# One core, cross attention and a binary-weight FFN in fp32: the FFN steps, the value products and the rotations in another order within a slot

## The reference

```python
q = (query @ Wq) ; k = (key @ Wk) ; v = (value @ Wv)      # query = layernorm(x), key = value = ctx
q = q * cos + _rotate_half(q) * sin                       # rotary, the same for k
attn = softmax(where(mask == 0, -1e9, q @ k.T / sqrt(128)))
x = x + (attn @ v) @ Wo
# FFN on y = layernorm(x)
routing = softmax(y @ gate_w.T)                           # 8 experts
in_scale, out_scale = routing @ in_channel_scale, routing @ out_channel_scale
x = x + (y * in_scale @ sign(weight).T * out_scale + bias)
```

## Time and profile before

| | us |
|---|---|
| median of 3 runs | 1142.5 |
| lowest, highest | 1142.41, 1143.6 |
| the profiled execution | 1143.86 |
| its span, first to last instruction | 1142.1 |
| PE busy in the span | 1131.5 |
| DVE, POOL, ACT busy | 814.2, 704.8, 537.4 |

### The profile page before, as it was taken

One profiled execution on the slowest core, in us unless ns is written; L12 is line 12 of the kernel. 1 busy time (PEld: TensorE's weight loads), 2 busy tenths in 40 slices (PEclk: granted clock), 3 DMA queues, 4 the chain that ended last, 5 costly groups with the idle time before them and its releaser, 6 DMA issues.

```text
span 1142.1 us, 22918 instructions
## 1 busy us (share of the span) xinstructions
PE 1131.5 (99%) x7927; PEld 954.3 (84%) x7927; DVE 814.2 (71%) x1366; ACT 537.4 (47%) x1736; POOL 704.8 (62%) x585
## 2 busy tenths in 40 slices
PE   8999999999999999999999999999999999999998
PEld 8788888888888888888888888888888888888877
DVE  5876877667677766877767776677766767776577
ACT  4554453544444354454554435544444544445533
POOL 5856676655667556675565676566674656755544
PEclk9999999999999999999999999999999999999999
DMA  8323342233323123332422323333232222322301
GB/s 250 113 80 98 106 133 84 83 102 89 97 69 113 61 92 94 105 116 88 115 86 69 99 81 87 91 106 107 84 93 74 75 85 73 89 77 74 93 20 38
DMA packets 134483, 105.29 MB, mean 92 GB/s; under 512 B 10680, under 2 KB 109256, under 8 KB 134400
## 3 DMA queue, kind: packets, MB, share of 16 engines
q1 hardware_dynamic: 128848, 93.72, 28.0%
q10 hardware_dynamic: 4784, 8.40, 2.2%
q0 software_dynamic: 768, 2.10, 0.6%
HBM read 100.00 MB, written 4.19 MB: 91 GB/s over the span
## 4 chain that ended last, share of the span: by engine, by line
PE 92%; DVE 3%; issue 2%; ACT 1%; POOL 1%; DMA 1%; ACTq 0%; DVEq 0%; POOLq 0%
PE chunk L1262 22%; PE chunk L1264 21%; PE chunk L1263 21%; PE duo_ps L1339 6%; PE o_ps L1362 3%; PE duo_ps L1251 2%; PE aux L1251 2%; PE duo_ps L1362 2%; DVE swp L945 1%; PE chunk L1315 1%; PE o_ps L1317 1%; PE o_ps L1316 1%; PE chunk L1317 1%; PE o_ps L1315 1%; PE chunk L1316 1%
## 5 line engine op out<-in xcount | busy, mean ns | idle before, releaser
L455 POOL TENSOR_TENSOR w_lo<-raw,w_hi 128x512 fp32r<-128x512 f32 x192 | 247.6, 1303 | 313.5 <-ACT w_hi L597 311.3
L945 DVE TENSOR_TENSOR swp<-chunk,sinT 64x512 f32<-64x512 f32 x320 | 220.2, 688 | 49.5 <-PE chunk L1264 29.9
L597 ACT ACTIVATE w_hi<-raw 128x512 fp32r<-128x512 f32 x192 | 116.6, 630 | 269.1 <-PE chunk L1264 202.4
L1262 PE MATMUL chunk<-xT_hi,w_hi 128*128 128x512 f32 x508 | 205.0, 404 | 0.6 <-POOL w_lo L455 0.6
L1264 PE MATMUL chunk<-xT_hi,w_lo 128*128 128x512 f32 x508 | 198.7, 391 | 0.0
L1263 PE MATMUL chunk<-xT_lo,w_hi 128*128 128x512 f32 x508 | 198.1, 390 | 0.0
L1262 PE MATMUL chunk<-wo_hi,oT_hi 128*128 128x512 f32 x492 | 195.1, 396 | 0.2 <-DVE oT_lo L879 0.2
L1264 PE MATMUL chunk<-wo_hi,oT_lo 128*128 128x512 f32 x492 | 191.9, 390 | 0.0
L1263 PE MATMUL chunk<-wo_lo,oT_hi 128*128 128x512 f32 x492 | 191.7, 390 | 0.0
L634 ACT ACTIVATE probs<-scores,neg_max 128x64 f32<-128x64 f32 x512 | 170.4, 337 | 42.5 <-DVE neg_max L901 42.5
L462 POOL TENSOR_TENSOR qT<-qT,swp 128x512 f32<-128x512 f32 x127 | 164.1, 1300 | 35.9 <-DVE qT L947 35.3
(11 more groups left out here) (305 smaller groups left out, 2045.8 us busy)
## 6 DMA issues: line engine op xcount, KB each, us to landing
raw<-in_L_xattn_Wq SPq DMA_DIRECT2D x128, 256.0 KB, 2.8
raw<-in_L_xattn_Wo SPq DMA_DIRECT2D x128, 256.0 KB, 2.7
raw<-in_L_xattn_Wk SPq DMA_DIRECT2D x32, 256.0 KB, 2.8
raw<-in_L_xattn_Wv SPq DMA_DIRECT2D x32, 256.0 KB, 3.0
acc<-in_x ACTq DMA_DIRECT2D x14, 256.0 KB, 2.7
x_tile<-in_x SPq DMA_DIRECT2D x12, 256.0 KB, 2.9
c_tile<-in_ctx SPq DMA_DIRECT2D x12, 256.0 KB, 3.2
result<-y ACTq DMA_DIRECT2D x12, 256.0 KB, 2.0
```

The costliest lines, as they stand in the source:

```text
L455: nc.gpsimd.tensor_tensor(lo, raw[:, r, :], hi.bitcast(F32), ALU.subtract).then_inc(wsplit_lo, 1)
L597: return nc.scalar.activation(dst, src, ACT.Copy)
L945: last = nc.vector.tensor_tensor(swp[to, k, :], bank[of, :], sinT[to, here], ALU.mult)
L1262: nc.tensor.matmul(bank, a_hi, b_hi, start=opens and i == 0, stop=False)
```

## The change

On PE, an even slot did projection 2, the values, the routing transpose, projection 3, the in-scales, projection 4, the out-scales, the value rows' first half, the sign product, the second half. It now does projections 2 and 3, the routing transpose, projection 4, the values, the in-scales, first half, out-scales, second half, sign product. In odd slots the out-scale product stands right behind the in-scales and goes to the bank `o_ps[1]`, which the attention values used, so it waits for `out_lo` of tile 1; ACT copies it from there. The second bank of the value rows is `chunk[1]` in place of `o_ps[0]`, and in odd slots `out_proj(s, 0)` follows the scores.

On DVE, `v_lo_split` moves from the odd slot's beginning to the even slot's end; the odd tile's `f_stats` and `f_norm` move into the even slot, around `rotate(s, 1)`; in even slots `out_lo` stands behind all rotations; in odd slots with an FFN tile `rotate(s, 1)` stands behind `scale_in`; in slot 31 `rotate(s, 0)` stands ahead of `pT_lo_split`. On POOL, in even slots rotation sums and splits alternate, and `xs_lo_split` stands behind `split_lo(s, 9)`. At the start four of six idle products go, three `split_lo` go from POOL to DVE, and one value weight is loaded by ACT's queue in place of SP's. In the last attention `out_proj(s, 3)` is cut after two heads instead of three.

```diff
-        V_BANK, FIRST_V_BANK = [chunk[1], o_ps[0]], [chunk[0], sc_ps]
+        V_BANK, FIRST_V_BANK = [chunk[0], chunk[1]], [chunk[0], sc_ps]
...
                     rope_sum(s, 0)
                     split_lo(s, 6 if s.odd else 5)
+                    if s.ffn and not s.odd:
+                        f_root(f[0] + 1, in_slot)
                     rope_sum(s, 1)
-                    if not s.odd:
-                        split_lo(s, 6)
+                if s.proj and s.odd:
                     split_lo(s, 7)
-                if s.ffn:
-                    xs_lo_split(f[0], in_slot)
-                if s.proj:
+                    if s.ffn:
+                        xs_lo_split(f[0], in_slot)
                     split_lo(s, 8)
                     rope_sum(s, 2)
...
                 if s.proj and not s.odd:
+                    split_lo(s, 6)
+                    rope_sum(s, 2)
+                    split_lo(s, 7)
+                    rope_sum(s, 3)
+                    split_lo(s, 8)
+                    rope_sum(s, 4)
                     split_lo(s, 9)
+                    if s.ffn:
+                        xs_lo_split(f[0], in_slot)
                     split_lo(s, 10)
-                    rope_sum(s, 3)
-                    rope_sum(s, 4)
...
                 if s.odd:
-                    rotate(s, 0)
+                    if s.number != SLOTS - 1:
+                        rotate(s, 0)
                     if s.ffn:
                         route_lo(f[0], in_slot)
                     if s.intake:
                         x_lo_split(*t)
-                    rotate(s, 1)
+                    if not s.ffn:
+                        rotate(s, 1)
                     out_lo(s, 0)
                     out_lo(s, 1)
                     if s.ffn:
                         scale_in(f[0], in_slot)
+                        rotate(s, 1)
                     rotate(s, 2)
...
+                    if s.ffn:
+                        f_stats(f[0] + 1, f[1] + 1, in_slot)
                     rotate(s, 1)
                     if s.ffn:
-                        route_lo(f[0], in_slot)
+                        f_norm(f[0] + 1, f[1] + 1, in_slot)
                     if s.intake:
                         x_lo_split(*t)
                     rotate(s, 2)
+                    rotate(s, 3)
+                    if s.ffn:
+                        route_lo(f[0], in_slot)
+                    rotate(s, 4)
+                    if s.ffn:
+                        scale_in(f[0], in_slot)
                     out_lo(s, 0)
-                    if s.ffn:
-                        scale_in(f[0], in_slot)
-                    rotate(s, 3)
                     out_lo(s, 1)
...
                 if not s.odd:
-                    rotate(s, 4)
+                    v_lo_split(s, 0)
+                    v_lo_split(s, 1)
...
+                for n in range(WRING):
+                    dve.wait_ge(wsplit_hi, n + 1)
+                    lo_of(flat(w_lo[:, n, :, :]), raw[:, n, :], flat(w_hi[:, n, :, :])).then_inc(wsplit_lo, 1)
...
+            def t_out_scales_apart(s, f, b, bank):
+
+                pe.wait_ge(o_lo, (s.U - 1) * PAIRS + 2)
+                nc.tensor.matmul(bank[:, :], b.routeT, out_sc[:, :], start=True, stop=True).then_inc(osc_done, 1)
...
                 if s.odd:
+                    project(s, 1)
+                    values(s, 0)
+                    values(s, 1)
+                    if s.ffn:
+                        t_route(f, in_slot)
+                    project(s, 2)
+                    if s.ffn:
+                        t_in_scales(f, in_slot)
+                        t_out_scales_apart(s, f, in_slot, o_ps[1])
+                    project(s, 3)
                     project(s, 4)
+                    if s.ffn:
+                        t_product(f, in_slot)
                 else:
+                    project(s, 2)
+                    project(s, 3)
+                    if s.ffn:
+                        t_route(f, in_slot)
+                    project(s, 4)
+                    values(s, 0)
+                    values(s, 1)
+                    if s.ffn:
+                        t_in_scales(f, in_slot)
                     v_rows(s, 0)
-                if s.ffn:
-                    t_product(f, in_slot)
-                if not s.odd:
+                    if s.ffn:
+                        t_out_scales(f, in_slot)
                     v_rows(s, 1)
+                    if s.ffn:
+                        t_product(f, in_slot)
...
-                idle_products(6)
+                idle_products(2)
```

More of the change, by code:

```diff
@@ L379, in load_weights @@
                         sp.wait_ge(wsplit_lo, split_count(s, n) - RING)
-                    if is_proj(c):
+                    if s.first_proj and c == V_OWN:
+                        pass
+                    elif is_proj(c):
                         src = (wk_c[:, :, bass.ts(grp, D)] if c == 0 else
@@ L1063, in slot @@
                     return scales_lo()
-                if s.odd:
-                    even = Slot(s.q, s.g - 1, False, False, odd=0)
-                    v_lo_split(even, 0)
-                    v_lo_split(even, 1)
                 if s.intake:
@@ L1083, in slot @@
                 if s.odd:
+                    add_out(s, 0)
+                    soft_b(s, 0)
                     add_out(s, 1)
-                soft_b(s, 0)
-                add_out(s, 2)
-                add_out(s, 3)
-                soft_b(s, 1)
-                if not s.odd:
+                    add_out(s, 2)
+                    soft_b(s, 1)
+                    add_out(s, 3)
+                    if s.number == SLOTS - 1:
+                        rotate(s, 0)
+                else:
+                    soft_b(s, 0)
+                    add_out(s, 2)
+                    add_out(s, 3)
+                    soft_b(s, 1)
                     rotate(s, 0)
@@ L1279, in out_proj @@
                     pe.wait_ge(added, (s.U - 3) * PAIRS + p + 1)
+                elif p < 2 and s.odd:
+                    pe.wait_ge(v_ok, s.U + p)
                 elif p == 0:
                     pe.wait_ge(cos_done, (s.U - 1) * KQ + 3)
-                elif p == 1 and s.odd:
-                    pe.wait_ge(v_ok, s.U)
                 elif p == 1:
@@ L1453, in attend_last @@
                 probs_T(s, 0)
-                out_proj(s, 3, range(HG - 1))
+                out_proj(s, 3, range(HG // 2))
                 values(s, 0)
-                out_proj(s, 3, range(HG - 1, HG))
+                out_proj(s, 3, range(HG // 2, HG))
                 probs_T(s, 1)
@@ L1490, in slot @@
                 t, f = (job and job[0] for job in jobs_of(s)[:2])
-                out_proj(s, 0)
                 if not s.odd:
+                    out_proj(s, 0)
                     out_proj(s, 1)
@@ L1500, in slot @@
                 if s.ffn:
-                    t_f(f, in_slot)
+                    t_f(f, in_slot, s.odd)
                 if s.odd:
+                    out_proj(s, 0)
                     out_proj(s, 1)
```

63 lines of the change are left out of this document (28 added, 35 removed).

## The result

| | before | after |
|---|---|---|
| median of 5 runs each on the same chip, us | 1142.5 | 1148.07 |
| lowest, highest | 1142.33, 1143.6 | 1147.17, 1149.13 |
| the profiled execution, its span | 1143.86, 1142.1 | 1149.13, 1147.3 |

The ratio is 1.0049, with a 95% interval of [1.0038, 1.0061]: the changed kernel is slower by 5.6 us, beyond the 0.2% of the prediction's text. The forecast was 1147.3, with a range of 1144.4 to 1149.8. The spans of the two profiles differ by 5.2 us.

A forecast was written before the change was run, and what follows sets the result against it. PE's stream was taken to bound the kernel, so only its waits count: +7.2 (odd slots) - 0.6 (even) - 0.6 (start) - 1.2 (end) = +4.8 us on 1142.5, giving 1147.3, range 1144.4 to 1149.8.

The forecast's parts named there:

- Odd slots, the largest term: Odd FFN slots: sign product waits for in-scales, scale_in, moved rotation and three POOL operations; 1.2 us each, +7.2 in six.
- makes projection 4 wait for the rotation of head 1, which is about nothing: Odd FFN slots: rotation ready at 390.93 against projection 4's start at 390.94, so taken as 0.
- Even slots with an FFN tile: Waits and returns saved (-0.22, -0.2) against new waits (+0.1, +0.2): -0.1 us a slot, -0.6 in six.
- Slots without an FFN tile: 0: Order changes, but no wait before and over 1 us of room in the same chains: 0.
- The return into the projections: Even FFN slots: in-scales right behind the values save one such return on PE, 0.2 us.
- The start: Program start: fewer idle products let first keys start sooner, partly at slow pace; -0.6 us, bounds 0 and 1.0 of gain.
- they stay covered: Start: DVE splits push x's statistics by about 2 us, hidden since PE transposes x only after 36 value matmuls.
- The end: Slot 31 and last attention: rotate(s, 0) in DVE's idle time gains 1.0, earlier out_proj cut 0.2; -1.2 us.
- lose the race to POOL: Even-slot rival: POOL's sum goes before f_norm, in-scales come 1.0 us later, six slots add 6.0; 1153.3 us, chance 0.15.
- The faster rival: Odd slots: the sign product does not wait, leaving -3.0; 1139.5 us, chance 0.10.
- The half wait: Odd slots: PE reaches the product later for other reasons, +3.6 instead of +7.2; 1143.7 us, chance 0.10.
- The start at the lower pace: Start rival: twelve key matmuls at the lower clock level, +1.1 instead of -0.6; 1149.0 us, chance 0.07.

The follow-up runs named there:

- experiment 1: Changed kernel with POOL doing split_lo 7 and xs_lo_split ahead of rope_sum 1 in odd slots with an FFN tile: 1141.03 us.
- experiment 2: Changed kernel with rotate(s, 1) of odd FFN slots back ahead of the two out_lo: 1146.48 us.
- experiment 3: Changed kernel with split_lo 8 also ahead of xs_lo_split on POOL in odd FFN slots: 1160.03 us.
- experiment 4: Kernel before with only the odd FFN slot's tail changed: rotate(s, 1) behind scale_in, out-scales behind in-scales in o_ps[1]'s bank: 1151.03 us.
- Experiment 10: Kernel of experiment 1 with the value weight's load on SP's queue and, in even FFN slots, xs_lo_split ahead of split_lo 9: 1139.23 us.
- experiment 8: Kernel of experiment 1 with the whole start of the kernel before (idle products, splits on POOL, load on SP's queue): 1141.38 us.
- experiment 9: Kernel of experiment 1 with the last slot's rotate(s, 0) back behind the routing: 1142.21 us.
- experiment 5: Kernel of experiment 1 with the first load of the own value weight back on SP's queue: 1140.33 us.
- experiment 12: Changed kernel with split_lo 8 and rope_sum 2 both ahead of xs_lo_split in odd FFN slots: 1170.97 us.
- experiment 6: Kernel of experiment 1 with the first three split_lo back on POOL instead of DVE: 1141.31 us.
- experiment 7: Kernel of experiment 1 with six idle products ahead of the first keys instead of two: 1141.2 us.

## Why the prediction was right, and where it was not

**Odd slots, the largest term: right in mechanism, 1 us too small.** Predicted 6 x 1.2 = +7.2, measured 6 x 1.37 = +8.2. The mis-sized term is the hand-overs from engine to engine: 0.25 in the sum, and 0.04, 0.03, 0.14 and 0.15 in the rows, 0.36 in all, the two at POOL the long ones. With it the chain from the in-scales to the product is 7.50 us, where the sum had 7.41 (387.48 to 394.89). Another 0.07 lies behind the product: its first step is 0.31 instead of 0.23. Beside this one step of the text failed without being paid for here: "makes projection 4 wait for the rotation of head 1, which is about nothing". Two times that agreed to 0.01 us were in truth a wait of 0.22: the matmul came 0.13 us behind the end of the rotation, and both the step to it and the one behind it were 0.1 too long. The chain covers this wait in the changed kernel; experiment 1 pays it, 6 x 0.24 = 1.4 us. Experiments 1 to 4 show the chain from each side.

**Even slots with an FFN tile: right**, -0.6 predicted and -0.7 measured. Experiment 10 shows that the wait for `xs_l` in it was real, at the 0.2 predicted.

**"Slots without an FFN tile: 0": wrong by a little.** The nine even ones behind the start are shorter by 0.05 to 0.09 us, 0.7 in all. The return into the projections that was counted in slots with an FFN tile is part of it: in slot 4 three projections in one piece take 8.38 us, where they took 8.52 in two pieces. The first keys of slot 2 and of the next slot start at 70.68 and 107.01 before, at 70.29 and 106.53 after: 36.33 and 36.24 apart.

**The start: its size is near, its reasoning failed.** Predicted -0.6; the two profiles reach the first keys of slot 2 (70.68 and 70.29) 0.39 apart, and by experiments 1 and 8 the start is worth 0.35. The step that failed is "they stay covered". It counted the splits on DVE, which push the statistics back, but not the DMA that the change puts ahead of x tiles 0 and 2 on ACT's queue. Nor was the profile of before a typical start: with the same code, experiment 4 gets out of it 1.5 us sooner (69.22). The gain was sooner keys and no wait for lo parts, the loss a pause at x of up to 1.1 us.

**The end: right**, -1.2 predicted and -1.1 measured (from the last projecting slot's keys to the end 67.45 before and 66.36 after, by spans of 1142.06 and 1147.32); experiment 9 gives the rotation's part, 0.86 in the pause.

Sum of the profiles: +8.2 - 0.7 - 0.7 - 0.4 - 1.1 = +5.3, against +4.8 predicted and 5.2 between the spans.

**The rivals.** `f_norm` did not lose the race to POOL in any even slot: it took 0.54 in all six. The faster rival, in which the product does not wait, did not come. Experiment 1 made it true and landed at 1141.0, where this rival had 1139.5: it took 0.1 off each odd slot, and projection 4's wait adds 0.24. The half wait did not come either. The start at the lower pace did not decide the profiled execution of the changed kernel, whose first four keys took 1.20 us; it exists in part in the profile of the kernel before (1.67), and in full in those of experiments 5 and 9 (2.08).

## What to carry to other kernels

When an operation is moved behind another on one engine, look at what the next engine's fixed order has queued behind its partner. Here POOL idled 3.17 us in front of a sum that nobody needed yet, with an operation behind it whose inputs became ready in that time and for which PE then stood still; putting this one first was worth 7 us. And a chain that ends within a few hundredths of the time at which PE arrives is not free: here it cost 0.1 to 0.2 us a time. An edit to a queue of loads at the start must be read by what stands behind it in that queue.

## What was not expected of the hardware

- PE standing still has a second price. Pauses of 0.9 us left the granted clock at 1.00 in the changed kernel. Behind pauses of 2.15 us it fell to the lower level in four of six slots, behind pauses of 3.4 us in all six, by the windows of experiments 3 and 12. It cost 1.3 to 1.6 us each time. Why equal pauses of 2.15 us differ is open. The Trainium skill, page "TensorE: Matmul & The Clock Gate", Part 1, has the clock fall when the engine has been idle; the windows agree.
- At the program's start the pace of matmuls differs from one execution to the next with the same code (four key matmuls in 1.19 us in experiment 1 and in 2.08 in experiment 9, which starts in the same way), while the granted clock reads 1.00 in both. The times of most of these kernels are spread over 2 to 3 us, more than most of the start's edits are worth. Most of this seems to arise at the start: in the profiles of experiments 1 and 5 to 8, which share the rest of the code, the first keys of slot 2 start at 68.26 to 70.11 us, and from there to the end it takes 1069.9 to 1070.2 in each. How much of the spread is the pace and how much are waits is not shown.
- Where DVE and POOL met, the one that began second paid: `f_norm` 1.49 us instead of 0.55 when POOL was first, POOL's sum 1.46 instead of 1.29 when DVE was. The Trainium skill, page "SBUF — State Buffer", section "SBUF: two separate sides", states this as a rule: of a POOL instruction and a DVE instruction that needs the ports the two share, whichever starts first holds them for its whole length. The two rows agree on who pays; POOL's 0.17 is less than the 0.31 us in which its row overlaps `f_norm`'s (347.63 to 347.94).
